# A graph network's kernel: the last attention group's logits later, 19 turned tiles copied by the vector engine, step tables of 16 bits

## The reference, cut to what matters

```python
h = relu(layernorm(x))
for i in range(3):
    h = segment_sum((h * out_norm)[src], dst) * in_norm
    h = h @ W[i] + b[i]            # relu but for the last
x1 = x + h
h = relu(layernorm(x1))
def gat_conv(x, src, dst, W, att_src, att_dst, bias, n_nodes):
    h = (x @ W).reshape(n, 4, 64)
    alpha = leaky_relu((h * att_src).sum(-1)[src] + (h * att_dst).sum(-1)[dst])
    e = exp(alpha - segment_max(alpha, dst)[dst])
    w = e / clip(segment_sum(e, dst), 1e-16)[dst]
    return segment_sum(w[:, :, None] * h[src], dst).reshape(n, 256) + bias
out = x1 + gat_conv(relu(gat_conv(h)))
```

## Time and profile before

| | |
|---|---|
| three runs, median (lowest, highest) | 6783.42 us (6779.98, 6793.79) |
| span of the profiled execution, first to last instruction | 5649.0 us |
| its own time | not given apart; the runs lie 1131 to 1145 us above the span |
| busy in the span | PE 4218.4, POOL 4159.4, DVE 3705.7, ACT 2101.0 us |
| mean granted clock of TensorE | 0.767 of full |
| chain that ended last | PE 40%, POOL 20%, DMA 14%, issue 11%, DVE 10%, ACT 5% |

### The profile page before, as it was taken

How to read it: one execution, slowest core, us unless ns; L and a number is a source line. 1 busy time by engine, 2 the same in 40 slices (tenths; PEclk the granted TensorE clock), 3 DMA queues, 4 the chain that set the end, 5 groups by cost and what they waited for, 6 DMA issues and landing times.

```text
span 5649.0 us, 84292 instructions
## 1 busy us (share of the span) xinstructions
PE 4218.4 (75%) x14997; PEld 2470.4 (44%) x14997; DVE 3705.7 (66%) x12168; ACT 2101.0 (37%) x7038; POOL 4159.4 (74%) x4290
## 2 busy tenths in 40 slices
PE   8677777777777778677777777777777677777772
PEld 7433333343333335333333355555554455555551
DVE  7555555555555554555555568777777677777777
ACT  4000000020000003000000088888887688888881
POOL 8677777777777777777777747777776677777776
PEclk7777677787777668777777778878888888888886
DMA  2443333333333333433333354444444344444444
GB/s 94 117 111 106 106 105 106 105 108 106 106 105 105 105 106 100 131 105 105 106 106 106 106 167 110 110 110 110 110 111 125 99 110 110 110 110 110 110 112 151
DMA packets 309459, 625.61 MB, mean 111 GB/s; under 512 B 85044, under 2 KB 180264, under 8 KB 308937
## 3 DMA queue, kind: packets, MB, share of 16 engines
q0 software_dynamic: 192928, 530.18, 33.3%
q1 hardware_dynamic: 109656, 88.65, 5.0%
q10 hardware_dynamic: 6384, 1.39, 0.1%
HBM read 573.37 MB, written 47.33 MB: 110 GB/s over the span
## 4 chain that ended last, share of the span: by engine, by line
PE 40%; POOL 20%; DMA 14%; issue 11%; DVE 10%; ACT 5%; POOLq 0%; DVEq 0%; SPq 0%; ACTq 0%
PE main L1071 20%; POOL ring L667 13%; PE main L1174 11%; DMA ring<-conv_tab,csrc 9%; DMA ring<-attn_tab,sidx 5%; POOL ring L679 5%; DVE acc L1365 3%; PE main L990 3%; POOL ring L699 2%; PE pso L1094 2%; ACT ring L912 2%; DVE ring L1226 1%; ACT oh L890 1%; DVE ad L1584 1%; PE pso L982 1%
## 5 line engine op out<-in xcount | busy, mean ns | idle before, releaser
L667 POOL DMA_INDIRECT ring<-conv_tab,csrc x2346 | 2222.6, 947 | 749.2 <-issue 590.4
L1071 PE MATMUL main<-ring,oh 128*128 x4992 | 2207.0, 565 | 758.2 <-DVE acc L1365 325.1
L1365 DVE TENSOR_TENSOR acc<-acc,main 128x264 f32 (+2 forms) x4160 | 1761.8, 424 | 1254.2 <-PE main L1071 1157.6
L679 POOL DMA_INDIRECT ring<-attn_tab,sidx x1664 | 1590.8, 956 | 604.5 <-issue 361.7
L1071 PEld LDWEIGHTS main<-ring,oh 128*128 128x128 f32 x4992 | 1092.0, 259 | 1869.7 <-issue 1801.3
L1174 PE MATMUL main<-ring,oh 128*128 128x264 f32 x3328 | 1246.2, 491 | 120.6 <-ACT ring L912 69.2
L912 ACT ACTIVATE ring<-ring 128x64 f32<-128x64 f32 x3328 | 910.9, 343 | 0.0
L1357 DVE TENSOR_SCALAR oh<-iota,dloc 128x128 f32<-128x128 f32 x2505 | 814.8, 325 | 91.9 <-issue 79.6
L1174 PEld LDWEIGHTS main<-ring,oh 128*128 128x128 f32 x3328 | 619.3, 229 | 290.3 <-DVE ring L1690 222.8
L890 ACT ACTIVATE oh<-iota,dloc 128x128 f32<-128x128 f32 x1664 | 528.9, 394 | 3.4 <-DMA attn_tab<-oh 3.4
L1690 DVE TENSOR_TENSOR ring<-ring 128x128 f32<-128x128 f32 x1664 | 463.1, 284 | 0.0
(11 more groups left out here) (212 smaller groups left out, 2993.3 us busy)
## 6 DMA issues: line engine op xcount, KB each, us to landing
ring<-conv_tab,csrc POOLq DMA_INDIRECT x2346, 2.7
ring<-attn_tab,sidx POOLq DMA_INDIRECT x1664
ring<-attn_tab SPq DMA_DIRECT2D x14, 896.0 KB, 8.5
conv_tab<-oh SPq DMA_DIRECT2D x12, 896.0 KB, 4.0
flag_room<-start_rows SPq DMA_DIRECT2D x416, 8.0 KB
flag_room<-end_rows SPq DMA_DIRECT2D x416, 8.0 KB
x_tab<-acc SPq DMA_DIRECT2D x7, 896.0 KB
oh<-x_tab SPq DMA_DIRECT2D x7, 896.0 KB
```

Source lines behind the costliest of these rows:

```text
L667: pool.indirect_dma_start(ring3[:, c % U, 0:C], None, conv_tab[k], bass.IndirectOffsetOnAxis(ap=csrc[:, c:c + 1], axis=0)).then_inc(gather ...
L679: pool.indirect_dma_start(ring3[:, j, 0:TW], None, attn_tab[l], bass.IndirectOffsetOnAxis(ap=sidx[:, i * GB * G + j:i * GB * G + j + 1], a ...
L1071: nc.tensor.matmul(main[s % 4][:, 0:width], oh[:, (s % OHR) * P:(s % OHR + 1) * P], ring[:, bass.ds(slots[s % 8], width)], start=True, sto ...
L1365: nc.vector.tensor_tensor(a, a, main[k][:, 0:width], ALU.add).then_inc(added, 1)
```

## The change

It has three parts.

- `step_words` and `step_tab` hold unsigned 16-bit words in place of 32-bit ones. The number of loads and the entries in each are the same.
- In the first attention table's stage, DVE copies the odd tiles from 11 to 47 (19 of 49) out of `pso`, in the iteration ten behind the tile's own; ACT keeps the others. PE's waits follow the two counters (`rows_turned`). The groups of `rstd` are finer at the start, and groups of seven have their root taken two tiles earlier on ACT; the reciprocal stands at iteration b+1 of DVE for a group that ends at b. The logit columns are read three iterations later.
- In the last group but one of each layer, the five parts and PE's five turns stand at steps 10, 11, 12, 13 and 15, and the folding and the first three weighings of the last group behind the sixteenth step.

```diff
-GROUPS = [(0, 2), (2, 7)] + [(a, a + 7) for a in range(7, 49, 7)]
+GROUPS = [(0, 2), (2, 4), (4, 7), (7, 10), (10, 14)] + [(a, a + 7) for a in range(14, 49, 7)]
+ROOT_AT = [a if b - a < 7 else a - 2 for a, b in GROUPS]
+TURNED = 10
+ON_DVE = [t >= TURNED and t % 2 == 1 for t in range(NT)]
...
-        step_words = dram("step_words", (4, SX), I32)
+        step_words = dram("step_words", (4, SX), U16)
...
+        PARTS_AT = (0, 3, 6, 9, 12)
+        LAST_PARTS_AT = (10, 11, 12, 13, 15)
+        TURNS_AT = (2, 5, 8, 11, G - 2)
+        LAST_TURNS_AT = (10, 11, 12, 13, 15)
...
+        def rows_turned(engine, m, t):
+
+            if t < 0:
+                past(engine, rows_T_copied, m * NT + t + 1 if m < HOPS else 0)
+            elif m == HOPS and ON_DVE[t]:
+                engine.wait_ge(odd_rows_copied, ODD_FROM + sum(ON_DVE[0:t + 1]))
+            elif m == HOPS:
+                engine.wait_ge(rows_T_copied, HOPS * NT + t + 1 - sum(ON_DVE[0:t + 1]))
...
@@ ACT, stage m == HOPS
-                if t + 1 < NT:
+                if t + 1 < NT and not ON_DVE[t + 1]:
                     copy_rows_T(3, t + 1)
                 for g in range(len(GROUPS)):
+                    if ROOT_AT[g] == t:
+                        root(rstd[:, GROUPS[g][0]:GROUPS[g][1]], 3 + g)
+                for g in range(len(GROUPS)):
                     if GROUPS[g][0] == t:
-                        root(rstd[:, GROUPS[g][0]:GROUPS[g][1]], 3 + g)
                         act.wait_ge(norm_ready, g + 1)
...
@@ DVE, stage m == HOPS
-                    if t == min(b + 1, NT - 1):
+                    if t == b + 1:
                         reciprocals(g)
-                if t >= 2 * TB and t % TB == 0:
+                if t >= TURNED and ON_DVE[t - TURNED]:
+                    copy_rows_T(HOPS, t - TURNED)
+                if t >= 2 * TB and t % TB == 3:
                     take_tv(0, t // TB - 2)
+            for t in range(NT - TURNED, NT):
+                if ON_DVE[t]:
+                    copy_rows_T(HOPS, t)
+                if t == ROOT_AT[-1]:
+                    reciprocals(len(GROUPS) - 1)
...
@@ DVE, attention
+                        before_last = it * GB + b == NG - 2
+                        part_at = LAST_PARTS_AT if before_last else PARTS_AT
...
-                            if k == G - LEAD and not last:
-                                fold_self(nb_, it * GB * 2 + 2 * (l * NG + b + 2),
-                                          bass.ds(it * GB * G + (b + 1) * G, G))
+                            if k == G - LEAD and not last and not before_last:
+                                open_group()
...
-                            if k == 0 and not last:
+                            if k == part_at[0] and not last:
                                 logits_part(it + over, nb_, c)
...
+                        if before_last:
+                            open_group()
+                            for k in range(LEAD):
+                                weigh(nb_, k)
```

More of the change, by code:

```diff
@@ L16 @@
 I32 = mybir.dt.int32
+U16 = mybir.dt.uint16
 ALU = mybir.AluOpType
@@ L351, in gnn @@
         nself = arrived[HOPS - 1]
+        odd_rows_copied = onehots
+        ODD_FROM = HOPS * (S + AHEAD)
         ARRIVALS, SLOT_AT, SUMS_AT, LOGITS_OF = range(4)
@@ L380, in staged_rows @@
             return room[:, at:at + width]
+        def rows_turned(engine, m, t):
[5 more added lines that the diff above has]
+                engine.wait_ge(rows_T_copied, HOPS * NT + t + 1 - sum(ON_DVE[0:t + 1]))
+            else:
+                engine.wait_ge(rows_T_copied, m * NT + t + 1 - (sum(ON_DVE) if m > HOPS else 0))
         def pool_gathers(k, c):
@@ L1175, in _ @@
                                              ring3[:, b * G + k, :], start=True, stop=True).then_inc(products_done, 1)
-                            if k == 2 and not last:
+                            turn_at = LAST_TURNS_AT if it * GB + b == NG - 2 else TURNS_AT
+                            if k == turn_at[0] and not last:
                                 turn_logits(c)
-                            if k == 5 and not last:
+                            if k == turn_at[1] and not last:
                                 turn_ends(c)
-                            if k == 8 and not last:
+                            if k == turn_at[2] and not last:
                                 turn_carries(c)
-                            if k == 11 and not last:
+                            if k == turn_at[3] and not last:
                                 turn_maxima(c)
-                            if k == G - 2 and not last:
+                            if k == turn_at[4] and not last:
                                 spread_factor(c, (b + 1) % GB)
```

23 lines of the change are left out of this document (13 added, 10 removed).

## The result

The change takes 6926.48 us, the median of four runs (6918.9 to 6936.04), against 6782.56 for the kernel before on the same chip: 143.9 us more, a ratio of 1.0209 with a 95% interval of 1.0195 to 1.0224. The forecast was 6793, the range ended at 6806. The profiled execution took 6936.04 us, 2.2 above its span of 6933.8. This alone breaks a step of the prediction: nothing of note lies outside a span. The trace of before (5649.0) and its runs (6783) came from different conditions, and the 1134 us between them must be inside the kernel.

A forecast was written before the change was run, and what follows sets the result against it. The row gathers on POOL were taken to bound the kernel, with PE, DVE and ACT having time to spare. Table stage +11.5 and tails -1.9 made +9.6: 6783.4 + 9.6 = 6793 us, range 6778 to 6806.

The forecast's parts named there:

- The baseline: Whole kernel: the 1,134 us by which the runs exceed the traced span lie outside it and carry over unchanged.
- Beside the gathers the register loads cost nothing: Hops and layers: register loads are hidden beside the gathers; only two loads of 16 values in each tail count.
- 16-bit tables, taken as 0, other end -2.0: Register loads in the tails: nothing if registers count, 0.5 us less a load, 2.0 in all, if bytes count.
- The table stage, +11.5: First attention table's building: PE's waits, slow clock and finer groups, less a gain of 4.3 us, make it 11.5 us longer.
- Tile 11: Table stage: PE waits 5.5 us for DVE's copy, as DVE is five tiles ahead, not ten.
- Clock: Table stage: after a 5.5 us gap PE runs two tiles at the lower clock, 2.0 us.
- rival 3: Table stage: PE's clock stays down behind the gap and later waits, +12.6 us in all, 6806 us; chance 0.16.
- Roots: Table stage: waits tied to ACT's roots, 1.9 us each at tiles 19 and 33, 1.2 at 27, 0.4 at 41; together 5.4.
- Columns: Table stage: logit column readings delay DVE's copies, 0.8 us each at tiles 15 and 29, 0.4 at 23 and 37; together 2.4.
- The gain: Table stage: with ACT freed of 19 copies, PE's pace of 1.13 us a tile saves 4.3 us of 47.2.
- Rivals 1 and 2: First: the copies are free, 6771 us, chance 0.10; second: no wait at tile 11 but at roots, 6783 us, 0.12.
- The tails, -1.9: Behind each layer's last gather: DVE's idle 3.23 and 2.32 us go, new waits cost 1.8 a layer; net -1.9 for both.

The follow-up runs named there:

- stand-in: Kernel before with only PE's arrival counts loaded as lower 16-bit halves of the 32-bit table: 5659.7 us, 1.0000; on a slower chip 6819.4 us, 1.0042.
- the stall: Kernel before, arrivals as 16-bit halves, plus two register loads in PE's queue every eight hop steps: 6994.3 us, 1.0232; with 16-bit tables 7439.0 us, 1.0878.
- the mended stage: Change's table stage alone, 32-bit tables, groups of three, DVE copying every third tile four iterations behind, against the kernel before: 5660.7 us, 0.9996.

## Why the prediction was wrong, and where it was right

**The baseline (failed).** The prediction said of the 1134 us that "nothing in the change touches what lies outside, and I carry it over". They did not lie outside. Where the kernel before takes 6780 us and more, the trace of its stand-in loses them inside: about half in the hops and their drains, where bursts in PE's queue are seen, and about half in the layers, where the cause is not. Spans and runs of one execution were 1.8 to 2.3 us apart. So the trace I argued from was one of a kernel in which PE had slack, and the runs I forecast were of one in which it had none: the last product 6 us behind the last gather in the one, 49 to 68 in the other, over all three hops.

**"Beside the gathers the register loads cost nothing" (failed).** This holds only with slack in PE's and DVE's queues. Measured: PE's narrow loads cost -0.3 us on chip two; on the slower kind of chip the arrivals' loads 31.8 us, and the rest of the words 143.9 - 48.5 = 95.4 us, 127 of the 144 in all. That sum is drawn across two groups of runs, on chips of one kind; no run there has the 16-bit tables alone without the stall. Measured within one group are the 31.8 us, the 16.7 of stage and tails, and, with the stall, 445 us for the words and 10 for stage and tails.

**16-bit tables, taken as 0, other end -2.0 (failed in sign).** Neither "bytes count" nor "registers count, nothing" holds. A load costs 0.59 us for 8 words of 32 bits and 1.10 for 16, that is 0.064 a register more, but 1.92 and 3.79 for words of 16 bits, 0.23 a register. The Trainium skill (Runtime: NRT & Kernel Launch, Instruction fetch mechanics) counts about 200 ns a register, for loads from HBM; these come from SBUF. The narrow loads come near it, the wide ones do not; I had set the rule aside because the row of the wide loads spoke against it. By it my estimate would have been 3.2 us for sixteen registers whatever the width; with that price on narrow words the tails would have been 2 x 2.1 us a layer dearer, and the hops' cost would still have been hidden in the trace I had. Even where there is slack, the words cost 5.6 us: behind the last gather DVE has two loads of 3.6 us in place of 1.1, of which the first falls partly into the wait for the last gathers.

**The table stage, +11.5 (right, in part by luck).** Measured +13.3 in the time and 12 to 14 in the gap. Tile 11: 5.5 predicted, 5.25 seen (the terms written out add up to 5.6 - 0.3 = 5.3). Clock: two slow tiles, 2.13 and 1.68 us for four passes against 1.06; the product of tile 15 takes 1.16 us again, so rival 3 (the clock stays down) did not come. The stage's row on chip two, which answers to the second of the earlier trace rows, has a granted clock of 0.90 where it was 0.96. Roots: 1.9 predicted for tiles 19 and 33, 1.66 seen at 19; 1.2 for tile 27, 0.96 seen. Columns: 0.8 for tile 15, 0.53 seen. Each wait was put some 0.25 too high: eight waits come to 11.0 us where the terms had 13.3. The gain was put too high by as much. Two lines of the earlier trace rows's view, beside the product at 3264.86 shown there:

```profile
3263.66 1.14 PE L990 MATMUL main<-wcat,aT 128*128 128x264 f32 x4
...
3266.05 1.15 PE L990 MATMUL main<-wcat,aT 128*128 128x264 f32 x4
```

Where PE waits for nothing, one tile's product starts 1.19 to 1.20 us behind the last; 1.13 was the distance of two transposes at one place. From tile 10 to 48 that makes 38 x 1.19 = 45.2 us, which is also what the mended stage takes in its trace. So of the 47.2 only 2.0 could be gained, not 4.3. These two errors cancel. The clock's 2.0 came as 1.9, the finer groups' 0.5 as 0.9, and about 1.2 us lie around the waits, which no term had. Rivals 1 and 2 fell with tile 11. The stage's row on chip two:

```profile
3238.00:3330.00 92.00, 70.32 (x310) 51.12 (x310) 58.33 (x214) 55.76 (x148) 1.50 (x2) 0.90 0.53 173
```

**The tails, -1.9 (the gain did not come).** Measured +1.3 with 32-bit tables (14.6 - 13.3, from two chips and within their uncertainty); by the traces the stretches behind the two layers grew from 116.3 and 121.3 us (stand-in) to 116.7 and 122.2. That is 238.9 us in all, where the seven traces with the old tails and 32-bit words for DVE have 237.5 to 239.4: neither a gain nor a loss can be told. The range's end of +1 was mis-worked, too: waits half as long again make 5.4 - 5.55 = -0.1. DVE's idle times in the second layer, stand-in first, then the change with 32-bit tables:

```profile
5529.31 0.62 DVE L1585 TENSOR_TENSOR ad<-ad 128x128 f32<-128x128 f32 x2 [2.25 <-DMA ring<-attn_tab,sidx]
```

```profile
5562.08 0.43 DVE L1389 TENSOR_TENSOR acc<-acc,main 128x264 f32 x1 [0.39 <-issue]
5563.72 0.43 DVE L1389 TENSOR_TENSOR acc<-acc,main 128x264 f32 x1 [1.21 <-PE main L1197]
...
5567.20 0.43 DVE L1389 TENSOR_TENSOR acc<-acc,main 128x264 f32 x1 [1.79 <-PE main L1197]
5569.02 0.43 DVE L1389 TENSOR_TENSOR acc<-acc,main 128x264 f32 x1 [0.25 <-issue]
```

The 2.25 us in front of the logits are gone, as predicted. The waits for PE's answers were put at 1.8 us, 0.6 and 0.9 of them before two adds. The two that end with a product are 1.21 and 1.79 us; for the other two, 0.39 and 0.25, the profile shows no releaser. I had priced PE's answer at the products' fast pace (0.56 us each). Here a product stands alone between two turns, and takes twice that:

```profile
5560.71 1.18 PE L1197 MATMUL main<-ring,oh 128*128 128x264 f32 x2
...
5562.34 1.25 PE L1197 MATMUL main<-ring,oh 128*128 128x264 f32 x2
```

The mean granted clock is 0.63 in these 15 us (5557 to 5572) and 0.89 in the same stretch of the stand-in (5526 to 5541): PE had sat idle 2.14 us before the logits' turn and 1.12 before the ends'. So parts that stand one step apart cost in two ways: DVE waits for an answer each time, and PE gives it at the lower clock. With 16-bit tables the tails cost 9.9 - 5.6 = 4.3 us over the words in the time, again within the uncertainty, and 3.1 us behind the layers by the traces (247.7 against 244.6); that the first narrow load already fills the wait that the ten earlier steps were to fill is argued, not shown.

**The chances.** 0.24 stood on slower by over 0.2%: 0.16 for the clock, which did not do it, and 0.08 for a sum that is short. It was short, by a term taken as nothing and a baseline taken from elsewhere, and no rival had either. On the chips where my trace holds, the change costs 21.1 us, 0.39%: inside the range by a little (its end is +22.6), outside the forecast of +3 to +14. Of it the stage makes 13.3 and the words 5.6; the rest is tails and what the two do to each other.

**Left open.** Why PE's queue issues in bursts of 0.70 us an instruction on some chips. SP's queue shows slow instructions too (up to 1393 ns in a wait of 17). What makes the layers longer there is open as well. Each chip served one group of runs, so chip and hour cannot be told apart. The transfers that bring in instructions look alike in both kinds of trace (some 0.3 to 0.7 us for 8 KB), and so do the gathers' landings (their last packet 1.4 us behind the gather's end in the median). A supply of instructions that now and then falls behind would fit, also with the stall's loads costing only a tenth of their time and taking the place of the bursts, but no run shows it.

## What to carry to other kernels

Hold a span against the runs before arguing from a trace: if they are hundreds of microseconds apart, the trace's slack is not that of the timed kernel, and everything costed at nothing "beside other work" has to be priced again without that cover. Price the register loads by word width: keep tables that engines load registers from in 32-bit words. When work is moved to another engine, ask how far that engine must be ahead, and which reply it waits for on the way: 19 copies ten tiles behind cost thirteen microseconds, 14 copies four tiles behind, with roots and reciprocals placed to suit, cost nothing. And take an engine's pace from many repetitions: one distance read at one place (1.13 us for 1.19) doubled the gain.

## What the runs showed of the hardware

A register load of 16-bit words takes three times as long as one of 32-bit words (1.92 against 0.59 us for eight registers, 3.79 against 1.10 for sixteen), the same in every trace, and also where the halves of 32-bit words are read. The kernel before ran 1120 to 1180 us apart on different chips (5659 to 5662 us in three groups of runs, 6783 to 6839 in three), with the same program and, in its own timed runs, a mean granted clock of 0.76 to 0.78 against 0.72 to 0.73. On the slower kind, 1198 us of added loads in the queue of the engine that held up the hops cost some 120 us, and most of that queue's slow instructions were gone (562 to 80); the next 415 us cost 398 in the hops. In the table stage and in the tails PE's clock fell behind idle times: four passes of a product took 2.13 us behind 5.25 us of idle time, 1.06 later, and one product 1.2 us behind idle times of 2.1 and 1.1, 0.56 where three follow each other.
